# Attention scores of two key tiles by 512 queries: seven products in two PSUM banks in place of eight

## What is computed

```python
# layer 0: dense attention, the adjacency matrix is added twice to the scores
q = x @ Wq.T + bq; k = x @ Wk.T + bk; v = x @ Wv.T + bv
a = q @ k.T * scale + adj + adj
x = layernorm(x + softmax(a) @ v)
# layer 1: graph attention, 8 heads of 64; mask = -1e10 * (1 - adj)
feats = einsum('nf,hfd->hnd', x, W)
dense = leaky(e_self[:, :, None] + e_neigh[:, None, :]) + mask
out = relu(concat_heads(softmax(dense) @ feats) + b)
x = layernorm(x + out)
```

## Time and profile before

| | us |
|---|---|
| median of 3 runs | 1752.93 (1752.52 to 1756.13) |
| profiled execution, whole | 1743.96 |
| its span | 1742.1 |
| PE busy | 1632.4 (94% of the span) |
| DVE busy | 1228.1 (70%) |
| POOL busy | 737.1 (42%) |
| ACT busy | 495.3 (28%) |
| mean granted clock of PE | 0.975 |

### The profile page before, as it was taken

The page is one execution under the profiler, slowest core; times in us unless marked ns, Lnnn a source line. Parts: engine busy times, 40 slices in busy tenths (PEclk is TensorE's granted clock), DMA queues, the critical chain, the costliest instruction groups (busy, mean ns, idle before and its releaser), DMA issues.

```text
span 1742.1 us, 22066 instructions
## 1 busy us (share of the span) xinstructions
PE 1632.4 (94%) x7748; PEld 748.8 (43%) x7748; DVE 1228.1 (70%) x2191; ACT 495.3 (28%) x765; POOL 737.1 (42%) x667
## 2 busy tenths in 40 slices
PE   8989999999999999999999999999999999999830
PEld 3334344444444444444444444444444444444310
DVE  4343255788897889787977797888877887854155
ACT  5334200222222223222222222222322222234326
POOL 2000000545444645464445444554455444558743
PEclk9999999999999999999999999999999999999965
DMA  6443533554556555555455455545555545436348
GB/s 217 145 169 121 178 100 121 161 190 155 181 161 213 162 176 164 186 189 173 160 194 187 157 185 179 197 153 172 168 211 166 184 153 182 157 100 222 131 136 293
DMA packets 150480, 298.25 MB, mean 171 GB/s; under 512 B 16352, under 2 KB 16352, under 8 KB 147424
## 3 DMA queue, kind: packets, MB, share of 16 engines
q1 hardware_dynamic: 147808, 288.42, 49.9%
q0 software_dynamic: 2560, 8.39, 1.6%
HBM read 253.76 MB, written 42.99 MB: 170 GB/s over the span
## 4 chain that ended last, share of the span: by engine, by line
PE 81%; DVE 8%; POOL 4%; ACT 3%; issue 2%; DMA 1%; SPq 0%; ACTq 0%; DVEq 0%; POOLq 0%
PE S L488 38%; PE O L545 32%; PE O L488 6%; PE X L488 3%; POOL ring L470 2%; POOL sacc L450 1%; POOL ring L442 1%; DVE xT L786 1%; DVE xr L914 1%; ACT xT L670 1%; DVE ring L871 1%; DVE cidx L849 1%; DVE cand L847 1%; PE X L587 1%; DVE xr L930 1%
## 5 line engine op out<-in xcount | busy, mean ns | idle before, releaser
L545 PE MATMUL O<-vring,ring 128*128 128x512 f16 x3072 | 704.5, 380 | 3.1 <-POOL ring L442 3.0
L488 PE MATMUL S<-yb,xT 128*128 128x512 f16 x3072 | 701.9, 380 | 4.1 <-DVE ring L877 4.1
L442 POOL TENSOR_TENSOR ring<-pf,ring 128x512 f16<-128x512 f32 x256 | 295.8, 1155 | 900.8 <-ACT ring L670 900.8
L488 PEld LDWEIGHTS S<-yb,xT 128*128 128x128 f16 x3072 | 301.0, 98 | 371.0 <-issue 7.1
L545 PEld LDWEIGHTS O<-vring,ring 128*128 128x128 f16 x3072 | 299.6, 98 | 358.0 <-issue 7.4
L721 ACT ACTIVATE pf<-ring 128x512 f32<-128x512 f32 x256 | 161.2, 630 | 994.8 <-DVE ring L871 969.3
L450 POOL TENSOR_TENSOR sacc<-sacc,pf 128x512 f32<-128x512 f32 x248 | 330.0, 1331 | 0.0
L877 DVE TENSOR_TENSOR ring<-S,ring 128x512 f32<-128x512 f32 x256 | 175.9, 687 | 179.3 <-PE S L488 172.4
L889 DVE TENSOR_TENSOR mx<-mx,ring 128x512 f32<-128x512 f32 x248 | 215.5, 869 | 8.5
L847 DVE MAX8 cand<-piece 128x8 f32<-128x512 f32 x256 | 174.8, 683 | 23.4 <-DMA piece<-in_adj 22.8
L871 DVE TENSOR_TENSOR ring<-BC,ring 128x512 f32<-128x512 f32 x256 | 172.2, 679 | 9.9 <-PE BC L571 9.9
(11 more groups left out here) (104 smaller groups left out, 714.1 us busy)
## 6 DMA issues: line engine op xcount, KB each, us to landing
ring<-in_adjT SPq DMA_DIRECT2D x256, 256.0 KB, 3.1
vring<-v_scratch SPq DMA_DIRECT2D x256, 256.0 KB, 2.7
piece<-in_adj SPq DMA_DIRECT2D x256, 256.0 KB, 3.7
ring<-in_xT SPq DMA_DIRECT2D x8, 1024.0 KB, 7.3
v_scratch<-vring SPq DMA_DIRECT2D x32, 256.0 KB, 2.2
y_scratch<-yb SPq DMA_DIRECT2D x8, 1024.0 KB, 4.9
yb<-y_scratch SPq DMA_DIRECT2D x8, 1024.0 KB, 7.0
xr<-in_x SPq DMA_DIRECT2D x32, 256.0 KB, 4.8
```

The costliest lines, as they stand in the source:

```text
L442: pool.tensor_tensor(ring16[:, e % SLOTS, 1, :], pf[:, e % NPF, :], ring16[:, e % SLOTS, 0, :], ALU.subtract).then_inc(lo_done, 1)
L488: mm = pe.matmul(psum, sta(a, k), mov(b, k), start=(k + a + b == 0), stop=(k == n - 1 and a == 1))
L545: mm = pe.matmul(O[j][:, :], ring16[:, e % SLOTS, a, j * P:(j + 1) * P], vring[:, e % NV, m, :], start=(k + a + m == 0), stop=(k == NT - 1 ...
```

## The change

Two key tiles (256 keys) by 512 queries over 512 features are now one **pair**: a 2 by 2 by 2 block product (keys halves of 128, feature halves of 256, query halves of 256), made with seven products for eight by the Strassen-Winograd scheme. In the prologue POOL makes sums of key blocks (s1 to s4, `key_sums`) and of query blocks (`query_sums`), which are then split into float16 parts as well. Three of the key sums stay in SBUF; a11, a12, a22 and s4 of a pair are written to DRAM (`x_scratch`) and loaded again for each block of queries, 512 KB per pair (`load_pair`, three buffers).

A product is six matmuls of 256 columns. Four products (`chain`) grow in bank S0 without being restarted and DVE reads the bank after each; three (`side`) use bank S1 (the first starts it, the second starts it anew, the third grows on it) and are read likewise. A read adds the bank to one quarter (128 keys by 256 queries) of the pair's two adj tiles in `ring`. The next product of a bank waits until the read before it is done. So a pair has seven DVE reads of 256 columns (`read_chain`, `read_side`) where two tiles had two adds of 512.

A step now is one pair and two value tiles, LAG is 18 steps, `ring` has 39 slots. PE alternates the products with halves of value tiles. Further:

- The scan runs MAX8 alone on each piece. After eight pieces `scan_row` finds the winning piece, POOL gathers it again from DRAM by row (`gather_piece`), and five pieces later `find` runs FIND_INDEX8 once on the gathered piece.
- Pieces per step follow a table (`piece_load`): 1 share at steps with remainder 2 to 8 by 16, else 3 shares; 226 shares carry the 256 pieces. A step's pieces are dealt to two places of the step (`scans(0)`, `scans(1)`), the first half or the larger part first.
- The four row tiles of layer 1 follow each other one step apart; normalising moves from DVE to ACT with two more small POOL operations; the bias of v is added in the prologue and no longer to x on POOL; the feature rows are evicted into `xr`.
- The last four row tiles are written as a pipeline of their own, and the proof is made while values still run.

Cut to its core:

```diff
-    LAG = 34
...
+    LAG = 18
+    SLOTS = 39
+    NX = 3
...
     NSC = 3
...
+    FIND_AFTER = 4
...
+        def piece_load(s):
+            return 0 if not LAG <= s < NCP - 2 else 1 if 2 <= s % NP <= 8 else 3
         def pieces_at(s):
...
+            total = sum(piece_load(i) for i in range(STEPS))
+            before = sum(piece_load(i) for i in range(s))
+            return range(before * NT * NPC // total, (before + piece_load(s)) * NT * NPC // total)
+        CHAIN = (("a11", 0), ("s2", 4), ("s3", 5), ("a22", 6))
+        SIDE = (("a12", 1), ("s1", 3), ("s4", 2))
...
             def load_adj(c):
...
-                    sp.wait_ge(add_done, c - 3)
+                    p, second = divmod(c - 4, 2)
+                    if second:
+                        sp.wait_ge(side_read, 3 * p + 2)
+                    else:
+                        sp.wait_ge(chain_read, 4 * p + 1)
...
-                    sp.wait_ge(cidx_set, p - NSC + 1)
+                    sp.wait_ge(cand_set, p - NSC + 1)
                 sp.dma_start(piece[:, p % NSC, :], adj[t * P:(t + 1) * P, q * PW:(q + 1) * PW]
                              ).then_inc(piece_in[p % NSC], 16)
...
+            for s in range(STEPS + 6):
+                for h in range(2):
+                    e = 2 * (s - LAG) + h
+                    if 0 <= e < NC:
+                        sp.wait_ge(pv_done, e + 1)
+                        if e + NV < NC:
+                            load_v(e + NV)
+                    if 2 * s + h + 3 < NC:
+                        load_adj(2 * s + h + 3)
+                    if h == 0:
+                        for p in pieces_at(s + 1):
+                            load_piece(p)
+                if s + NX < NCP:
+                    sp.wait_ge(chain_done, 4 * (s + 1))
+                    load_pair(s + NX)
...
+            def key_sums(g):
...
+                    last = pool.tensor_tensor(s1, a21, a22, ALU.add)
...
+                    last = pool.tensor_tensor(s3, a11, a21, ALU.subtract)
...
+                    last = pool.tensor_tensor(sx[:, 1, t], sx[:, 0, t], a11, ALU.subtract)
...
+            def gather_piece(t):
...
+                pool.indirect_dma_start(out=won, out_offset=None, in_=adj.rearrange("n (q w) -> (n q) w", w=PW),
+                                        in_offset=bass.IndirectOffsetOnAxis(ap=wonrow[:, t % 2:t % 2 + 1], axis=0)
+                                        ).then_inc(won_in, 16)
...
+            def product(bank, p, keys, queries, start):
+                b = p // NP
+                for c in range(2):
+                    for a, m in ((0, 0), (0, 1), (1, 0)):
+                        mm = pe.matmul(bank, keys_of(p, keys, a, c), yb[:, b % 2, queries, m, c, :],
+                                       start=(start and c + a + m == 0), stop=(c == 1 and a == 1), skip_group_check=True)
+                return mm
...
+                if p + n >= 1:
+                    pe.wait_ge(chain_read, 4 * p + n)
+                product(chain, p, *CHAIN[n], n == 0).then_inc(chain_done, 1)
+            def side_product(p, n):
+                if p + n >= 1:
+                    pe.wait_ge(side_read, 3 * p + n)
+                product(side, p, *SIDE[n], n < 2).then_inc(side_done, 1)
...
+                    pe.wait_ge(rinv_set, b + 1)
+                elif b < NB - 1:
                     pe.wait_ge(f_set, t)
...
+            for s in range(STEPS):
+                e = 2 * (s - LAG)
+                scoring, multiplying = s < NCP, 0 <= e < NC
+                if scoring:
+                    chain_product(s, 0)
+                    side_product(s, 0)
                 for j in range(JB):
-                    b = block_at(s, 3 + 2 * j)
+                    b = block_at(s, 2 + j)
                     if b is not None:
                         transpose_x1(b * JB + j)
...
+                if scoring:
+                    chain_product(s, 2)
+                    side_product(s, 2)
+                for j in range(JB):
+                    b = block_at(s, 2 + j)
                     if b is not None:
                         feats(b * JB + j)
...
+                if multiplying:
+                    values(e + 1, 0)
+                    values(e + 1, 1)
...
+            def unit_rows(t, dst):
+                j = t % JB
+                act.wait_ge(scale_set, 4 * t + 4)
+                nc.scalar.activation(dst, xr[:, j, :], ACT.Identity, bias=nmean[:, j:j + 1], scale=rstd[:, j:j + 1]
...
-                part = piece[:, p % NSC, :]
-                dve.max(cand[:, q, :], part).then_inc(cand_set, 1)
-                wait_apart(cand_set, p + 1)
-                dve.max_index(cidx[:, q, :], cand[:, q, :], part).then_inc(cidx_set, 1)
+                dve.max(cand[:, q, :], piece[:, p % NSC, :]).then_inc(cand_set, 1)
...
                 wait_apart(cand_set, (t + 1) * NPC)
-                dve.max(top8[:, :], cf).then_inc(top_set, 1)
...
+                dve.max(top8[:, t % 2, :], cand[:, :, :].rearrange("p q k -> p (q k)")).then_inc(top_set, 1)
+                wait_apart(top_set, t + 1)
+                dve.max_index(wonq[:, t % 2, :], top8[:, t % 2, :], cand[:, :, 0]).then_inc(wonq_set, 1)
+                dve.wait_ge(wonq_set, t + 1)
...
+                dve.tensor_scalar(wonrow[:, t % 2:t % 2 + 1], wonq[:, t % 2, 0:1], rowf[:, :], float(t * P * NPC), ALU.add,
+                                  ALU.add).then_inc(wonrow_set, 1)
+                dve.tensor_copy(top2[:, t, :], top8[:, t % 2, 0:2]).then_inc(scan_set, 1)
+            def find(t):
+                wait_apart(won_in, (t + 1) * 16)
+                dve.max_index(wonidx[:, :], top8[:, t % 2, :], won).then_inc(wonidx_set, 1)
+                dve.wait_ge(wonidx_set, 2 * t + 1)
+                dve.scalar_tensor_tensor(out=pickf[:, :], in0=wonq[:, t % 2, 0:1], scalar=float(PW), in1=wonidx[:, 0:1],
+                                         op0=ALU.mult, op1=ALU.add).then_inc(wonidx_set, 1)
+                dve.wait_ge(wonidx_set, 2 * t + 2)
                 dve.tensor_scalar(pick[:, t:t + 1], pickf[:, :], float(N - 1), None, ALU.min).then_inc(scan_set, 1)
...
+            def quarter(p, key, query):
+                return ring[:, (2 * p + key) % SLOTS, query * QH:(query + 1) * QH]
+            def read_chain(p, n, key, query):
+                dve.wait_ge(chain_done, 4 * p + n + 1)
+                dst = quarter(p, key, query)
+                dve.tensor_tensor(dst, chain, dst, ALU.add).then_inc(chain_read, 1)
+            def read_side(p, n, key, query):
+                dve.wait_ge(side_done, 3 * p + n + 1)
+                dst = quarter(p, key, query)
+                dve.tensor_tensor(dst, side, dst, ALU.add).then_inc(side_read, 1)
...
+                dve.scalar_tensor_tensor(out=xr[:, j, :], in0=feats_bank(t), scalar=1.0 / (W_UP * X1_UP), in1=b1b[:, :],
...
+                if scoring:
+                    landed(2 * s)
+                    read_chain(s, 0, 0, 0)
+                    dve.wait_ge(chain_read, 4 * s + 1)
+                    read_side(s, 0, 0, 0)
+                if exponent:
+                    subtract(e)
+                for j in range(JB):
+                    b = block_at(s, 3 + j)
+                    if b is not None:
+                        evict_feats(b * JB + j)
+                if 1 <= s <= NCP:
+                    maximum(2 * s - 2)
+                if scoring:
+                    read_chain(s, 1, 0, 1)
+                    landed(2 * s + 1)
+                    read_side(s, 1, 1, 1)
+                if 1 <= s <= NCP:
+                    maximum(2 * s - 1)
+                for j in range(JB):
+                    b = block_at(s, 1 + j)
+                    if b is not None:
+                        unit_rows_lo(b * JB + j, xr[:, j, :])
+                if exponent:
+                    subtract(e + 1)
+                b, r = divmod(s, NP)
+                if r == 0 and 1 <= b <= NB:
+                    maxima(b - 1)
+                scans(0)
+                if scoring:
+                    dve.wait_ge(side_read, 3 * s + 2)
+                    read_chain(s, 2, 1, 1)
+                    dve.wait_ge(chain_read, 4 * s + 2)
+                    read_side(s, 2, 0, 1)
+                turning = block_at(s, -1, NB)
+                if turning is not None:
+                    inverse_sums(turning)
+                    evict(turning, 0)
+                    evict(turning, 1)
+                scans(1)
+                if scoring:
+                    read_chain(s, 3, 1, 0)
+                if turning is not None:
+                    evict(turning, 2)
+                    evict(turning, 3)
```

873 lines of the change are left out of this document (524 added, 349 removed).

## The result

The changed kernel takes **1922.8 us** (1920.7 to 1925.7), the kernel before 1752.7 in the same runs: a ratio of 1.097, 95% interval 1.0945 to 1.0989. It is 170 us slower; 58 were forecast, with a range that ended at 1848. The profiled execution took 1921.2 us, with a span of 1919.4.

A forecast was written before the change was run, and what follows sets the result against it. PE was taken to bound the main loop, busy 199.8 of 200 us. Profiled 1744 - 77 (PE's saving) + 118 (loop waits) + 20 (prologue) - 3 (tail) = 1802, plus 9: 1811 us; range 1755 to 1848.

The forecast's parts named there:

- A matmul of 256 columns, 0.108: PE's products: a 256-column matmul, not in the earlier trace, runs at its columns' speed, 0.108 us.
- A read, 0.41: DVE's 256-column bank reads take 0.41 us each, from a line between 64 and 512 columns.
- the rival with 0.15: PE's 256-column matmul with its weight load takes 0.15 us, total 1929 us; chance 3%.
- Transposes, 41 us for 21 tiles: Main loop, layer 1: PE's transposes wait for the previous tile's evict_feats, 1.94 us, 21 times: 41 us.
- The fourth piece, 47 us: Four-piece steps: with three buffers the fourth lands late, 1.5 us in 18 steps, 2.5 in 8: 47 us.
- SP's later issues: Sync engine's queue: values, an adj tile and keys held behind the fourth piece are due a step later, costing nothing.
- row work, 24 us: Three-piece steps: scan_row and find cost 20 us ahead of read 3 in 17 steps, 4 us behind it in 8.
- plain MAX8, 1 us: Plain three-piece steps lose 0.2 us each at the fourth chain product: 8 steps, 1 us.
- prologue, +20 us: Start to step 18: POOL's sums, collisions and a late first read add 20 us; bounds +8 and +35.
- tail, -3 us: From last value to first gather: pipelined feats save 3 us; the 32 gathers stay.
- That DVE keeps PE fed: Main-loop rival: reads come earlier, the fourth piece is in time, only transposes wait: 1734 us, faster; chance 17%.
- More collisions: Main-loop rival: DVE waits more for POOL, 0.3 us in 110 steps, 33 us: 1844 us; chance 12%.

The follow-up runs named there:

- e13: Changed kernel with late transposes, two prologue moves, two or three pieces a step, row work and FIND behind the fourth chain read; 1733.8 us, ratio 0.9898.
- e1: Changed kernel with the transposes of the unit rows behind the second side product instead of the first; 1884.4 us, ratio 1.0734.
- e14: Changed kernel, fourth piece not fetched in the 26 four-piece steps, its MAX8 rereading the third's buffer, general path left out; 1882.0 us.
- e3: Changed kernel with the next step's pieces issued behind the second adjacency and value tiles instead of ahead of them; 1920.8 us, ratio 1.0932.
- e6: Changed kernel without the scan's row work, pieces past the first three not fetched, all 256 MAX8 kept, general path left out; 1808.4 us.
- e4: Changed kernel with the scan left out (pieces, maxima, gathers, FIND) and the general path too; 1795.9 us, ratio 1.0235.
- e11: Changed kernel with four moves: late transposes, pieces spread evenly, last prologue stores first, value evictions ahead of query halves; 1794.0 us, ratio 1.0244.
- e8: Changed kernel with the next group's first two value-tile evictions ahead of this group's low query halves in the prologue; 1897.1 us, ratio 1.0894.
- e7: Changed kernel with the first key pairs, adjacency tiles and queries fetched behind the last prologue group's stores; 1903.2 us, ratio 1.0912.
- e17: e15 with first queries, two key pairs and four adjacency tiles fetched ahead of the last value tile's store; 1724.3 us, ratio 0.9836.
- e15: e13 with the fourth adjacency tile fetched beside the first three; 1729.4 us, ratio 0.9875.

## Why the prediction was off, point by point

The direction was right and the size was not: 112 us are missing from the sum. By the same clock it has 1802 where the profiled execution took 1921.2. Up to step 18 some 40 us are missing from it, from there to the end of the last score (1690.1, forecast 1595) 54, and behind that 24. **The steps that failed** are the loop waits of the scan (76 us forecast, 127 measured), the prologue (+20 forecast, +60 measured) and, in part, the tail.

- **Direction and mechanism** were right: PE's saving is real, and DVE's order takes it back. It shows where the waits are gone: the loop of e13 takes 1155.6 us; 109 steps of 9.71 and the transposes and feats of 24 tiles (2.59 + 0.45 each) are 1131. The remaining 24 fit the six block turns and 0.06 us a step; this is not taken apart.
- **A matmul of 256 columns, 0.108** (12 of them from 574.35 to 575.66 in e1, 0.109 each): right. **A read, 0.41**: 0.42 (the groups above), which is also what the formula of the Trainium skill, VectorE: DVE Perf Modes, gave. Both terms that no row of before showed were well taken, and the rival with 0.15 fell.
- **Transposes, 41 us for 21 tiles**: -41 by the ratio of e1, 30 in its loop. Only 18 of the tiles stand beside scores, at 2.04 each, and PE's 19 waits on `xr` are 34.0 us. The cost of one was right.
- **The fourth piece, 47 us**: -41 by e14, 38 in the loop. The size is near, in part by luck: the sum has all of it in the 26 steps of four pieces, whose own part is 20, and nothing in the steps behind.
- **Failed: "SP's later issues (...) are due a step later still, so they cost nothing."** DVE waited 47.7 us in the loop for adjacency tiles, which the forecast had at none, and e14, which lacks only the fourth transfers, has no such wait: the late tiles come with the fourth piece. That they are the other half of its gain is read from the waits; e3, tried for it, only moved part of the wait from the tile to the piece.
- **Mis-sized: row work, 24 us**, and 4 more in the one-share steps and turns: 51 in the loop, of which 33 lie in the steps of three pieces, 13 in those of four, where the sum has it only behind the fourth piece in 8 steps, and 5 in the one-share steps. The prediction's step by the clock gave DVE's two-input operations beside POOL their price once a step; in the step shown above `pickf` on one element takes 0.65 us since POOL started 0.63 before it, and the prediction had 0.15 to 0.2 for such. How much of the 51 this makes is not shown.
- **Mis-sized: plain MAX8, 1 us**: 12 in the loop (e6 against e4).
- **Failed: prologue, +20 us.** Step 18 begins at 359.9, forecast 319.5. The first read is 31 us late, since PE's last product ends 22 late (at 222.40) and the read follows it by 19.5 for a forecast of 11. 16 of the 31 go with the two moves (225.90 in e11): value evictions behind query halves (e8), and the store of a value tile behind the first scores' loads in the sync engine's queue (e7), at which the prediction did not look. 3.0 more go with the queries early (e17); the other 12 are not taken apart. Pairs alone were near at 5.85, but the first two steps took 7.8 and 11.7, the second for a tile 5.8 us late by queue order (e15).
- **In part failed: tail, -3 us.** From the end of the last score to the end of the span it is 229.3 us, 24 more than the sum has. 8.3 lie in the values alone: PE has 36.4 value tiles there for 34.9 before (3.9 us, which the sum counts in the loop), and 3.11 is one wait for a value tile. 6 lie between the last value (1811.9) and the first gather, 32.0 us for a forecast of 25.9; two products of layer 1 took 4.38 and 4.08 at granted clocks of 0.63 and 0.67, where before only the first was slow, with 4.60 at 0.59, and the next took 2.76 at 1.00. The last 10 lie behind the first gather, which starts 75.4 us before the span's end (before: 65.7). These are not the change's: e7 and e8, with the same tail, have 64.2 and 63.9. The 9 us that the forecast adds at its end, the kernel before's median over its profiled execution, are of the same size; that they are the same thing is likely and not shown. No run tried the tail.
- **The rivals.** That DVE keeps PE fed was given 17% and "it decides at 60 us of loop waits". As changed it was false; e13, which keeps all the work, shows that it is a matter of order and spread. Its "77 us by three items" are 118 less 41, but the three items add up to 72. "More collisions" had the right side and too small a size.

The scan's part of the loop is 64 + 51 + 12 for 47 + 28 + 1, in the order in which e4 to e6 take it apart.

## What to carry to other kernels

When two engines hand a bank to and fro, ask of each instruction on the reading engine not how long it takes but between which two reads it stands; work that is free in one gap costs PE its time in another, here some 60 us of 1923, on top of 70 for the uneven spread. Where a ring has fewer buffers than a step has pieces, the surplus piece's round trip is inside the step, and everything issued behind it in that queue waits as well (half of e14's 38 us lay in the steps behind), so spread the pieces before adding queues. Cost the queue of the engine that issues the transfers like a compute engine, at the seams between stages first.

## What was not expected of the hardware

- The queues carried 246 GB/s over 200 us at a share of 0.74, with PE busy 99.8% of them, where 209 at 0.62 had looked like a load that hurts.
- An operation on one element with two SBUF inputs took 0.65 us beside a POOL instruction (L1168 above), 4 times what the 128x1 TENSOR_SCALAR of the earlier trace rows took.
- From the first gather to the end of the span took 64.2 us in e7, 63.9 in e8 and 75.4 in the changed kernel, with the same instructions. In the last DVE stood idle there once for 7.2 us and ScalarE for 6.2 with nothing named that they waited for; e7 has no such idle time. No run tried what sets it.
